# Attention decoder layer: context turned by a DMA transpose per batch, and value products run in pairs

## The chip, the cores and the metric

One core of a Trainium2 chip runs the whole kernel as one program. The metric is the device time in microseconds, the median over several runs. A profile is one more execution, recorded by the hardware profiler.

## The reference

A decoder layer on 16 batches of 56 tokens with 128 features, each with a context of 1500 rows. Cut to what matters here:

```python
x = x + self_attention(layernorm(x))                       # 16 heads of 8
q = heads(layernorm(x) @ Wq.T);  k = heads(ctx @ Wk.T);  v = heads(ctx @ Wv.T)
scores = einsum('bhqd,bhkd->bhqk', q, k) / sqrt(8) + bias[:, None, None, :]   # 16 x 16 x 56 x 1500
x = x + merge(softmax(scores) @ v) @ Wo.T
x = x + experts(layernorm(x))                              # 32 experts, top 4, and a shared one
```

The change touches the cross-attention alone: how the context is turned so that TensorE can project keys and values from it, and in what order the loop over key tiles issues its work.

## The kernel before, in words

The program writes out each engine's instructions by hand, with semaphores between them. SP issues every DMA, on one queue. There are three stages. The first projects queries and keys of the self-attention and prepares batches 0 and 1 of the cross-attention; in it the self-attention runs over 16 batches (`self_step`). The second is the cross-attention, 16 iterations, one per batch (`iteration(r, c)`, batch 3r + c; TensorE, ScalarE, VectorE and SP have one each, batches 1 to 12 in a loop of four rounds of three). The third is the expert layer.

**Preparing a batch.** SP loads 1500 context rows as 12 tiles of 125 rows (`load_ctx`, 750 KB, three buffers). GpSimd (POOL) splits them into two half-precision parts, `ch` (L555 and L558, three buffers). Then nine uses of a PSUM bank follow: T0 to T2, TensorE transposes 2 x 4 blocks of 128 x 128 (`ctx_transpose`, L672) and VectorE copies the bank to `ct` (`take_ctx`, L1323, one buffer); K0 to K2, three matmuls of 500 columns project the keys (L339 to L341 through `split_matmul`), ScalarE copies one half (L1085), VectorE subtracts the other (L1330); V0 to V2, twelve matmuls of 128 columns, a copy by ScalarE (L1089). When K2 is read, SP spreads the keys over the row groups with 12 DMAs (`key_stacks`, L412; the four bias rows, L407, go ahead of them). Batches 0 to 2 are prepared in the first stage, with three banks; batches 3 to 15 in iterations 1 to 13, two batches ahead of use.

**A cross-attention iteration** has 12 steps, one for each tile of 125 keys. In a step TensorE does, in this order: the use of the one bank `misc` that the list `MISC` names for the step (L67: T, K, V, `sel` to pick the heads' outputs of the batch before, `mt` to transpose the maxima of the next batch, `tr` to transpose the result); the scores, four matmuls (L910); one matmul for the maxima of the next batch (L866); the value products of the tile before, eight matmuls in fp32 (`times_v`, L767 and L770); a second matmul for the maxima (L866). The next batch's maxima are computed ahead in 24 such products, over two banks (`mbank`), each reduced by VectorE (L1506); they become a row that is added to the scores. For that, TensorE transposes them (`mt`, L903), ScalarE copies the row (L1166), and SP writes it into the queries with a DMA (L462). The first scores of a batch wait for that DMA (`mrow_in`). The scores of a tile go to one of two banks (`sbank`), ScalarE takes the exponential into one of two buffers `p` (L1171, bias per key), and the value products read it. ScalarE does the `misc` use of a step first and the exponential after it; VectorE the `misc` use first and the two maxima after it.

**SP in an iteration** waits until POOL has split the batch three ahead, loads its context, waits for the scores of the last batch, loads the queries (L423) and stacks the keys of the batch two ahead, and sends the row of maxima.

Of the kernel before, what the change touches and what calls it, by code (L numbers as in the profile page):

```python
# [38 lines left out]
G = 4  # L39
# [23 lines left out]
PREP = ["T0", "T1", "T2", "K0", "K1", "K2", "V0", "V1", "V2"]  # L63
# [3 lines left out]
MISC = ["T0", "K0", "T1", "K1", "T2", "K2", "sel", "V0", "V1", "V2", "mt", "tr"]  # L67


TAIL = {(B - 2, "T0"): "out", (B - 2, "K2"): "norm", (B - 1, "T0"): "logits"}  # L70
OFFSET = {"T": 2, "K": 2, "V": 2, "s": -1, "t": -1, "m": 1}
# [13 lines left out]
def used(r, c, use):  # L85

    return (prep_live if use[0] in "TKV" else live)(r, c + OFFSET[use[0]]) or tail(r, c, use) is not None
# [7 lines left out]
def misc_index(r, c, use):  # L95

    if not isinstance(r, int) and c < 1:
        return misc_index(r, c + 3, use) - 3 * len(MISC)
# [3 lines left out]
    return n if isinstance(r, int) else n + 3 * len(MISC) * r  # L102

# [34 lines left out]
def build(nc, x_d, ctx_d, bias_d, qkv_w, qkv_b, proj_w, proj_b, wq, wk, wv, wo,  # L138
          wg, w1, w2, w3, ws1, ws2, ws3, out_d):
    with ExitStack() as stack:  # L140
# [49 lines left out]
        ch = [sb(f"ch{n}", [128, 2, KT, D], F16) for n in range(3)]  # L190
        ct = sb("ct", [128, 2, KT, 128], F16)
# [7 lines left out]
        p = [sb(f"p{n}", [128, H * S], F32) for n in range(2)]  # L199
        mx = sb("mx", [112, 8, 3], F32)  # L200
# [84 lines left out]
        prep_read = {u: sem(f"prep_read{u}") for u in "TKV"}  # L285
# [11 lines left out]
        ch_ok = sem("ch_ok")  # L297
        k1_ok = sem("k1_ok")
# [55 lines left out]

        def use_bank(r, c, j):
# [8 lines left out]
        def _(sp):  # L364
# [26 lines left out]

            def query_stacks(n, k):
# [34 lines left out]
            query_stacks(0, 0)  # L427
            query_stacks(0, 1)
# [3 lines left out]
            load_ctx(0, 3)  # L432
            sp.wait_ge(mselfr_ok, 1)
# [4 lines left out]

# [30 lines left out]
            with sp.Fori(0, 4, 1) as r:  # L469
# [40 lines left out]
        def _(pool):  # L510
# [32 lines left out]
            def split_ctx(r, c):  # L543
# [5 lines left out]
                if not isinstance(r, int) or b >= 3:  # L549

                    if isinstance(r, int):
                        pool.wait_ge(*use_filled(r, c - 3, "T2"))
                    else:
                        pool.wait_ge(misc_done, misc_index(r, c - 4, "T0"))
                nc.gpsimd.tensor_tensor(ch[n][:, 0], ctx[n][:], zero[:].to_broadcast([128, KT, D]), ALU.add  # L555
                                        ).then_inc(ch_step, 1)
                pool.wait_ge(ch_step, b + 1)
                nc.gpsimd.tensor_tensor(ch[n][:, 1], ctx[n][:], ch[n][:, 0], ALU.subtract).then_inc(ch_ok, 1)  # L558
# [71 lines left out]
        def _(pe):  # L630
# [30 lines left out]
            def ctx_transpose(r, c, j):  # L661

                if not early(r, c):
                    pe.wait_ge(misc_read, batch_index(r, c, f"T{j}"))
                elif 3 * r + c:
                    pe.wait_ge(*use_read(r, c - 1, f"V{j}"))
                pe.wait_ge(ch_ok, 3 * r + c + 1)
                bank = use_bank(r, c, j).bitcast(F16)
                for part in range(2):
                    for t in range(4):  # L670
                        o = 512 * part + 128 * t
                        last = tr(bank[:, o:o + 128], ch[c % 3][:, part, 4 * j + t], identh[:])  # L672
                last.then_inc(use_filled(r, c, "T0")[0], 1)

            def key_project(r, c, j):

                if early(r, c):
                    pe.wait_ge(*use_read(r, c, f"T{j}"))
                else:
                    pe.wait_ge(misc_read, batch_index(r, c, f"K{j}"))  # L680
                c1, c2 = ct[:, 0, 4 * j:4 * j + 4, 0:KP], ct[:, 1, 4 * j:4 * j + 4, 0:KP]
# [4 lines left out]
            def value_project(r, c, j):  # L686
# [4 lines left out]
                for t in range(4):  # L691
                    last = split_matmul(use_bank(r, c, j)[0:KP, 128 * t:128 * t + 128],
                                        ct[:, 0, 4 * j + t, 0:KP], ct[:, 1, 4 * j + t, 0:KP],
# [3 lines left out]
            prepare = {"T": ctx_transpose, "K": key_project, "V": value_project}  # L697
# [38 lines left out]
            for use in PREP[0:6]:  # L736
                prepare[use[0]](0, 0, int(use[1]))
# [7 lines left out]
            for use in PREP[6:]:  # L745
# [4 lines left out]
            for use in PREP[0:3]:  # L750
                prepare[use[0]](0, 1, int(use[1]))
# [5 lines left out]
            for use in PREP[3:]:  # L757
# [88 lines left out]
            for use in PREP[0:6]:  # L846
# [22 lines left out]
            def pv_tile(r, c, t):  # L869
# [3 lines left out]
                if t == 0:  # L873
# [3 lines left out]
                    else:  # L877
                        pe.wait_ge(misc_read, misc_index(r, c, "T0"))
                    pe.wait_ge(o_read, B + 3 * r + c)
                times_v(v[c % 3][:, t], p[t % 2], KP, t == 0, t == KT - 1)  # L880

            def iteration(r, c):
                for s in range(KT):
                    use = MISC[s]
                    if used(r, c, use):
                        if use[0] in "TKV" and not tail(r, c, use):
                            prepare[use[0]](r, c + 2, int(use[1]))
                        else:
                            pe.wait_ge(misc_read, misc_index(r, c, use))
                        if tail(r, c, use) == "out":  # L890
                            out_project(1, 0, misc, misc_done)
                        if tail(r, c, use) == "norm":
                            transpose_norm(2, 0, 6, misc_done)
                        if tail(r, c, use) == "logits":
                            router_logits(0, misc).then_inc(misc_done, 1)
                        if use == "sel":
                            pe.wait_ge(o_read, B + 3 * r + c)
                            pick_heads()
                        elif use == "tr":
                            tr(misc[:, 0:128], tok[:], ident[:]).then_inc(misc_done, 1)  # L900
                        elif use == "mt":
                            pe.wait_ge(mcol_ok, 3 * r + c + 2)
                            tr(misc[0:8, 0:112], mcol[:], ident[0:112, 0:112]).then_inc(misc_done, 1)  # L903
                    if live(r, c):
                        if s == 0:
                            pe.wait_ge(mrow_in[c % 3], 16 * (r + c // 3 + 1))

                        pe.wait_ge(exp_done, B + KT * (3 * r + c) + s - 1)
                        for g in range(G):
                            last = mm(sbank[s % 2][0:KP, g // 2, 224 * (g % 2):224 * (g % 2) + 224],  # L910
                                      ks[c % 3][0:ROWS, g, KP * s:KP * s + KP],
                                      qsb[c % 3][0:ROWS, HG * g:HG * g + HG].rearrange("p h q -> p (h q)"),
                                      start=True, stop=True)
                        last.then_inc(st_done, 1)
                    (off0, k0), (off1, k1) = chunks(s)
# [692 lines left out]
```

## Time and profile before

| | |
|---|---|
| Time, median of 3 runs | 643.82 us (643.49 to 644.13) |
| Profiled execution: span of its instructions | 640.8 us |
| Share of the span in which TensorE is busy | 89% |
| VectorE | 71% |
| ScalarE | 53% |
| GpSimd | 25% |
| Mean granted TensorE clock | 0.928 |
| Mean DMA traffic | 70 GB/s |

The profiled execution counts from its first instruction to its last; the measured time holds some 3 us more, around the span. Matmuls are pipelined: the length of one in the trace is longer than the distance between two, so what an instruction costs TensorE is read from the starts. SPq is the queue of SP, and its lengths are those of the issue, not of the transfer. A line in brackets after an instruction says how long its engine was idle before it and what ended that.

### The profile page before, as it was taken

How to read it: one execution, taken by the hardware profiler on the slowest of the kernel's cores; microseconds unless marked ns; L12 is line 12 of the kernel's file. 1: busy time of each engine (PE TensorE's matmuls, PEld its weight loads, DVE VectorE, ACT ScalarE, POOL GpSimd, SP SyncE). 2: the span in 40 equal slices, each digit the busy share in tenths (PEclk: the TensorE clock that was granted, in tenths of full speed). 3: DMA queues.
4: the chain of work that ended last, by engine and by line, in shares of the span. 5: the costliest groups of instructions: out<-in, count | busy, mean ns of one | idle time of the engine just before them, and what ended most of it. 6: DMA issues, size and time to landing. Idle time of an engine off the chain costs nothing.

```text
span 640.8 us, 18136 instructions
## 1 busy us (share of the span) xinstructions
PE 569.6 (89%) x6656; PEld 368.7 (58%) x6656; DVE 458.0 (71%) x879; ACT 342.0 (53%) x509; POOL 162.4 (25%) x105
## 2 busy tenths in 40 slices
PE   3588887588999997999979999799999999689996
PEld 2267665344676774767747677476776666334442
DVE  6954435977888784787747878488788873478885
ACT  2630654314666663666636666366666668235553
POOL 6895000400033033030330303303030004025540
PEclk9975999775999997999969999799999999789999
DMA  4473300143432432224322243222421304002200
GB/s 108 151 143 111 77 0 2 35 103 72 106 79 72 120 77 73 68 68 122 78 70 62 74 116 78 76 57 79 116 79 26 74 2 101 1 13 50 49 0 29
DMA packets 45473, 45.12 MB, mean 70 GB/s; under 512 B 30387, under 2 KB 37259, under 8 KB 45403
## 3 DMA queue, kind: packets, MB, share of 16 engines
q1 hardware_dynamic: 45403, 44.07, 26.2%
q8 instruction: 58, 0.95, 0.6%
q14 instruction: 12, 0.10, 0.1%
HBM read 16.82 MB, written 0.46 MB: 27 GB/s over the span
## 4 chain that ended last, share of the span: by engine, by line
PE 75%; DVE 8%; issue 6%; POOL 5%; DMA 2%; ACT 2%; SPq 1%; ACTq 0%; DVEq 0%; POOLq 0%
PE ps L866 16%; PE ps L767 12%; PE ps L910 11%; PE ps L339 6%; PE ps L340 5%; PE ps L341 5%; PE ps L672 4%; PE ps L975 3%; PE ps L770 3%; PE ps L777 2%; PE ps L729 2%; DVE mx L1506 2%; DMA ctx<-in_ctx 2%; PE ps L960 1%; DVE xn L1252 1%
## 5 line engine op out<-in xcount | busy, mean ns | idle before, releaser
L1506 DVE TENSOR_REDUCE mx<-ps 112x1 f32<-112x500 f32 x384 | 251.0, 673 | 54.3 <-PE ps L866 52.3
L1171 ACT ACTIVATE p<-ps,bres 125x896 f32<-125x896 f32 x192 | 193.1, 1006 | 92.7 <-PE ps L910 91.9
L866 PE MATMUL ps<-ks,qsb 97*112 97x500 f16 x384 | 160.4, 420 | 11.4 <-DVE mx L1506 10.9
L555 POOL TENSOR_TENSOR ch<-ctx,zero 128x1536 f16<-128x1536 f32 x16 | 43.9, 2745 | 286.2 <-DMA ctx<-in_ctx 286.2
L910 PE MATMUL ps<-qsb,ks 98*125 98x224 f16 x768 | 109.9, 266 | 0.0
L767 PE MATMUL ps<-p,v 125*27 125x168 f32 x1664 | 105.8, 322 | 4.4 <-issue 2.8
L910 PEld LDWEIGHTS ps<-qsb,ks 98*125 98x125 f16 x768 | 83.3, 140 | 14.3 <-issue 2.1
L866 PEld LDWEIGHTS ps<-ks,qsb 97*112 97x112 f16 x384 | 50.6, 132 | 41.5 <-DVE mx L1506 21.5
L767 PEld LDWEIGHTS ps<-p,v 125*27 125x27 f32 x1664 | 31.8, 105 | 59.7 <-issue 53.5
L770 PE MATMUL ps<-p,v 125*9 125x56 f32 x1664 | 60.5, 215 | 0.0
L770 PEld LDWEIGHTS ps<-p,v 125*9 125x9 f32 x1664 | 47.1, 92 | 11.1
L1330 DVE TENSOR_TENSOR k<-ps,k 128x500 f16<-128x500 f32 x48 | 32.4, 677 | 29.1 <-ACT k L1085 29.1
L558 POOL TENSOR_TENSOR ch<-ctx,ch 128x1536 f16<-128x1536 f32 x16 | 50.4, 3149 | 1.3
L1085 ACT ACTIVATE k<-ps 128x500 f16<-128x500 f32 x48 | 28.2, 588 | 36.5 <-PE ps L341 36.4
L672 PE MATMUL ps<-identh,ch 128*128 128x128 f16 x384 | 32.1, 236 | 15.1 <-issue 10.9
L1089 ACT ACTIVATE v<-ps 125x512 f32<-125x512 f32 x48 | 28.4, 596 | 27.9 <-PE ps L341 27.7
L1323 DVE COPY ct<-ps 128x1024 f16<-128x1024 f16 x48 | 32.6, 682 | 13.4 <-PE ps L672 13.2
L672 PEld LDWEIGHTS ps<-identh,ch 128*128 128x128 f16 x384 | 26.2, 107 | 23.7 <-issue 14.1
L339 PE MATMUL ps<-wt,ct 128*125 128x128 f16 x192 | 37.0, 227 | 0.0
L341 PE MATMUL ps<-wt,ct 128*125 128x128 f16 x192 | 36.9, 226 | 0.0
L340 PE MATMUL ps<-wt,ct 128*125 128x128 f16 x192 | 36.9, 226 | 0.0
L612 POOL TENSOR_TENSOR ks<-ks,zero 128x384 f16<-128x384 f32 x17 | 19.7, 1158 | 59.2 <-PE ps L975 40.4
(172 smaller groups left out, 799.9 us busy)
## 6 DMA issues: line engine op xcount, KB each, us to landing
ks<-k SPq DMA_DIRECT2D x192, 93.8 KB
ctx<-in_ctx SPq DMA_DIRECT2D x16, 750.0 KB
ks<-in_L_ffn_W SPq DMA_DIRECT2D x48, 64.0 KB, 2.0
qsb<-qs SPq DMA_DIRECT2D x15, 168.0 KB, 7.7
qs<-late SPq DMA_DIRECT2D x8, 168.0 KB, 4.1
ks<-brow SPq DMA_DIRECT2D x64, 2.9 KB
qs<-late SPq DMA_DIRECT2D x16, 56.0 KB, 2.9
qs<-late SPq DMA_DIRECT2D x8, 112.0 KB, 2.5
```

What stands on the lines that cost most here:

```text
L339: nc.tensor.matmul(out, a1, b1, start=True, stop=False)
L340: nc.tensor.matmul(out, a1, b2, start=False, stop=False)
L341: return nc.tensor.matmul(out, a2, b1, start=False, stop=True)
L555: nc.gpsimd.tensor_tensor(ch[n][:, 0], ctx[n][:], zero[:].to_broadcast([128, KT, D]), ALU.add).then_inc(ch_step, 1)
L558: nc.gpsimd.tensor_tensor(ch[n][:, 1], ctx[n][:], ch[n][:, 0], ALU.subtract).then_inc(ch_ok, 1)
L672: last = tr(bank[:, o:o + 128], ch[c % 3][:, part, 4 * j + t], identh[:])
L767: mm(obank[32 * quad:32 * quad + 27, 0:168], vt[0:keys, 27 * quad:27 * quad + 27], pt[0:keys, 168 * quad:168 * quad + 168], start=first, s ...
L770: done = mm(obank[32 * quad:32 * quad + 9, 168:224], vt[0:keys, 108 + 9 * quad:117 + 9 * quad], pt[0:keys, 672 + S * quad:672 + S * quad + ...
L866: mm(mbank[k % 2][0:112, 0:CH], qsb[n][0:ROWS - 1, 2 * pair:2 * pair + 2].rearrange("p h q -> p (h q)"), ks[n][0:ROWS - 1, pair // 2, CH * ...
L910: last = mm(sbank[s % 2][0:KP, g // 2, 224 * (g % 2):224 * (g % 2) + 224], ks[c % 3][0:ROWS, g, KP * s:KP * s + KP], qsb[c % 3][0:ROWS, HG ...
L1171: A(p[s % 2][0:KP].rearrange("p (a c) -> p a c", a=2), sbank[s % 2][0:KP, :, 0:448], ACT.Exp, scale=SCALE, bias=bres[:, bass.ds(i, 1), s:s ...
L1506: V.tensor_reduce(mx[:, k // 3, k % 3:k % 3 + 1], mbank[k % 2][0:112, 0:CH], axis=AX.X, op=ALU.max).then_inc(mx_read, 1)
```

## The change

The context is turned by one DMA per batch. `ctx_transpose` and `take_ctx` go, with the T uses of the `misc` bank. SP issues `dma_start_transpose` from `ch` to `ct`; `ct` has three buffers, `ch` one, so POOL splits a batch only when the transposition of the batch before has landed, and SP issues a transposition only when the last one has landed. In an iteration it stands behind the load of the queries and ahead of the key stacks, for the batch three ahead; the context load goes four ahead. SP's loop is written out. `MISC` keeps 12 places, three of them empty. Value products run in odd steps only, for the two tiles before the last one, with three buffers `p` (the third lies in `wnat`). In a step TensorE now does the value products, the scores, the first maxima product, the `misc` use and the second maxima product; ScalarE does the exponential before the `misc` use, VectorE the maxima before it.

```diff
-PREP = ["T0", "T1", "T2", "K0", "K1", "K2", "V0", "V1", "V2"]
+PREP = ["K0", "K1", "K2", "V0", "V1", "V2"]
-MISC = ["T0", "K0", "T1", "K1", "T2", "K2", "sel", "V0", "V1", "V2", "mt", "tr"]
+MISC = ["", "K0", "", "K1", "", "K2", "sel", "V0", "V1", "V2", "mt", "tr"]
...
-        ch = [sb(f"ch{n}", [128, 2, KT, D], F16) for n in range(3)]
-        ct = sb("ct", [128, 2, KT, 128], F16)
+        ch = sb("ch", [128, 2, KT, D], F16)
+        ct = [sb(f"ct{n}", [128, 2, KT, 128], F16) for n in range(3)]
...
+        p.append(wnat[:].rearrange("p n d -> p (n d)")[:, 0:H * S])
...
+            def transpose_ctx(r, c):
+                if not live(r, c):
+                    return
+                n, b = c % 3, 3 * r + c
+                sp.wait_ge(ch_ok, b + 1)
+                if not isinstance(r, int) or b > 0:
+                    sp.wait_ge(*ct_landed(r, c - 1))
+                if isinstance(r, int) and 3 <= b < 3 + EARLY:
+                    sp.wait_ge(*use_filled(r, c - 3, "V2"))
+                elif not isinstance(r, int) or b >= 3:
+                    sp.wait_ge(misc_done, misc_index(r, c - 3, "K0"))
+                sp.dma_start_transpose(out=ct[n][:].rearrange("p a t k -> p (a t) k"),
+                                       in_=ch[:].rearrange("p a t d -> p (a t d)")).then_inc(ct_ok[n], 16)
...
             query_stacks(0, 0)
+            transpose_ctx(0, 0)
             query_stacks(0, 1)
...
             key_stacks(0, 0)
             load_ctx(0, 3)
+            transpose_ctx(0, 1)
...
             key_stacks(0, 1)
+            transpose_ctx(0, 2)
...
# SP, iteration(r, c)
-                if not isinstance(r, int) or 3 * r + c >= 1:
-                    load_ctx(r, c + 3)
+                if not isinstance(r, int) or 3 * r + c >= 0:
+                    load_ctx(r, c + 4)
                 if prep_live(r, c + 2):
                     sp.wait_ge(st_done, B + KT * (3 * r + c))
                     load_queries(r, c + 2)
+                if not isinstance(r, int) or 3 * r + c >= 0:
+                    transpose_ctx(r, c + 3)
+                if prep_live(r, c + 2):
                     key_stacks(r, c + 2)
...
-            with sp.Fori(0, 4, 1) as r:
+            for r in range(4):
...
# POOL, split_ctx
+                if not isinstance(r, int) or b > 0:
+                    pool.wait_ge(*ct_landed(r, c - 1))
...
# TensorE
-            for use in PREP[0:6]:
+            for use in PREP[0:3]:
                 prepare[use[0]](0, 0, int(use[1]))
...
             self_maxima(0)
-            for use in PREP[0:3]:
-                prepare[use[0]](0, 1, int(use[1]))
...
             def iteration(r, c):
                 for s in range(KT):
+                    (off0, k0), (off1, k1) = chunks(s)
+                    if s % 2:
+                        for t in (s - 3, s - 2):
+                            if live(r, c if t >= 0 else c - 1):
+                                pv_tile(r, c if t >= 0 else c - 1, t % KT)
                     if live(r, c):
+                        scores(r, c, s)
                     if live(r, c + off0):
                         max_chunk(r, c, off0, k0)
-                    if s == 0 and live(r, c - 1):
-                        pv_tile(r, c - 1, KT - 1)
-                    if s > 0 and live(r, c):
-                        pv_tile(r, c, s - 1)
+                    misc_use(r, c, s)
                     if live(r, c + off1):
                         max_chunk(r, c, off1, k1)
...
# ScalarE, iteration: now ahead of the misc use
+                    if live(r, c):
+                        tile = B + KT * i + s
+                        act.wait_ge(st_done, tile + 1)
+                        act.wait_ge(pv_done, tile - 2)
+                        A(p[s % 3][0:KP].rearrange("p (a c) -> p a c", a=2), sbank[s % 2][0:KP, :, 0:448],
...
+                    if s == 1 and live(r, c - 1):
+                        act.wait_ge(pv_done, B + KT * i)
+                        A(osb[:], obank[:, 0:224], ACT.Copy).then_inc(o_read, 1)
```

## Rows read from the trace of the kernel before

**Rows 1.** The chain that ended last, shares of the span by line.

```profile
PE ps L866 16%; PE ps L767 12%; PE ps L910 11%; PE ps L339 6%; PE ps L340 5%; PE ps L341 5%; PE ps L672 4%; PE ps L975 3%; PE ps L770 3%; PE ps L777 2%; PE ps L729 2%; DVE mx L1506 2%; DMA ctx<-in_ctx 2%; PE ps L960 1%; DVE xn L1252 1%
```

**Rows 2.** Busy time by stretch: length, busy per engine, clock, DMA share, GB/s.

```profile
171.00:195.00 24.00, 23.91 (x347) 16.52 (x340) 19.50 (x35) 15.45 (x22) 5.86 (x2) 1.00 0.32 90
...
322.10:354.40 32.30, 27.81 (x341) 18.06 (x340) 19.67 (x34) 15.53 (x21) 5.84 (x2) 0.84 0.24 68
...
378.60:403.20 24.60, 24.60 (x349) 17.15 (x349) 20.08 (x36) 16.14 (x23) 5.86 (x2) 1.00 0.32 88
```

**Rows 3.** Timeline of PE, two steps: start us, length us, instruction, count, [idle before].

```profile
303.34 0.62 PE L672 MATMUL ps<-identh,ch 128*128 128x128 f16 x8
...
303.79 0.55 PE L910 MATMUL ps<-qsb,ks 98*125 98x224 f16 x4
...
304.18 0.38 PE L866 MATMUL ps<-ks,qsb 97*112 97x500 f16 x1
...
304.49 0.49 PE L767 MATMUL ps<-p,v 125*27 125x168 f32 x8
...
304.79 0.28 PE L770 MATMUL ps<-p,v 125*9 125x56 f32 x8
...
305.00 0.42 PE L866 MATMUL ps<-ks,qsb 97*112 97x500 f16 x1
...
305.26 0.38 PE L339 MATMUL ps<-ct,wt 128*128 128x500 f16 x1
...
305.90 0.55 PE L910 MATMUL ps<-qsb,ks 98*125 98x224 f16 x4
...
307.45 0.62 PE L672 MATMUL ps<-identh,ch 128*128 128x128 f16 x8
```

**Rows 4.** Timeline of VectorE and ScalarE in the same two steps.

```profile
304.48 1.01 ACT L1171 ACTIVATE p<-ps,bres 125x896 f32<-125x896 f32 x1 [1.01 <-PE ps L910]
...
304.97 1.25 DVE L1506 TENSOR_REDUCE mx<-ps 112x1 f32<-112x500 f32 x2
...
306.10 0.59 ACT L1085 ACTIVATE k<-ps 128x500 f16<-128x500 f32 x1 [0.61 <-PE ps L341]
...
306.72 0.68 DVE L1330 TENSOR_TENSOR k<-ps,k 128x500 f16<-128x500 f32 x1 [0.50 <-ACT k L1085]
```

**Rows 5.** Timeline of ScalarE in batch 0, steps without preparation.

```profile
164.45 1.01 ACT L1171 ACTIVATE p<-ps,bres 125x896 f32<-125x896 f32 x1 [0.46 <-PE ps L910]
165.91 1.01 ACT L1171 ACTIVATE p<-ps,bres 125x896 f32<-125x896 f32 x1 [0.46 <-PE ps L910]
```

**Rows 6.** Timeline around the row of maxima, PE, ScalarE and SP's queue.

```profile
311.54 9.12 SPq L412 DMA_DIRECT2D ks<-k  x12
...
320.10 0.26 PE L903 MATMUL ps<-ident,mcol 112*8 112x112 f32 x1
...
320.40 0.25 ACT L1166 ACTIVATE mrow<-ps 8x112 f16<-8x112 f32 x1
...
320.77 0.68 SPq L462 DMA_DIRECT2D qsb<-mrow  x1
```

**Rows 7.** DMA queue, then issues: KB each, median us to landing.

```profile
q1 hardware_dynamic: 45403, 44.07, 26.2%
...
qsb<-qs SPq DMA_DIRECT2D x15, 168.0 KB, 7.7
...
qsb<-late SPq DMA_DIRECT2D x8, 14.0 KB, 1.8
```

**Rows 8.** Timeline of SP's queue and of PE, first stage.

```profile
31.30 1.28 SPq L400 DMA_DIRECT2D qs<-late  x2
...
54.90 0.48 SPq L386 DMA_DIRECT2D ctx<-in_ctx  x1
...
63.30 0.62 PE L339 MATMUL ps<-ct,wt 128*128 128x500 f16 x1
```

**Rows 9.** Timeline of SP's queue, end of the late query stacks.

```profile
163.58 1.70 SPq L400 DMA_DIRECT2D qs<-qd  x1
```

More of the change, by code:

```diff
@@ L85, in used @@
 def used(r, c, use):
-    return (prep_live if use[0] in "TKV" else live)(r, c + OFFSET[use[0]]) or tail(r, c, use) is not None
+    if not use:
+        return False
+    return (prep_live if use[0] in "KV" else live)(r, c + OFFSET[use[0]]) or tail(r, c, use) is not None
 def tail(r, c, use):
@@ L297, in build @@
         ch_ok = sem("ch_ok")
+        ct_ok = [sem(f"ct_ok{n}") for n in range(3)]
         k1_ok = sem("k1_ok")
@@ L659, in out_project, with key_project @@
                 last.then_inc(done, 1)
-            def ctx_transpose(r, c, j):
+            def key_project(r, c, j):
                 if not early(r, c):
-                    pe.wait_ge(misc_read, batch_index(r, c, f"T{j}"))
+                    pe.wait_ge(misc_read, batch_index(r, c, f"K{j}"))
                 elif 3 * r + c:
                     pe.wait_ge(*use_read(r, c - 1, f"V{j}"))
[L667 to L681, printed above, removed]
+                if j == 0:
+                    pe.wait_ge(*ct_landed(r, c))
+                c1, c2 = ct[c % 3][:, 0, 4 * j:4 * j + 4, 0:KP], ct[c % 3][:, 1, 4 * j:4 * j + 4, 0:KP]
                 out = use_bank(r, c, j)[:, 0:CH].rearrange("p (t k) -> p t k", t=4)
@@ L744, in _ @@
             last.then_inc(bt_psum, 1)
-            for use in PREP[6:]:
+            for use in PREP[3:]:
                 prepare[use[0]](0, 0, int(use[1]))
@@ L756, in _ @@
             tr(ps[:, 0, 0:112], mself[:].rearrange("p b k -> p (b k)"), ident[0:112, 0:112]).then_inc(mselft_psum, 1)
-            for use in PREP[3:]:
+            for use in PREP:
                 prepare[use[0]](0, 1, int(use[1]))
@@ L845, in _ @@
             pe.wait_ge(x_ok, 1)
-            for use in PREP[0:6]:
+            for use in PREP[0:3]:
                 prepare[use[0]](0, 2, int(use[1]))
@@ new lines, in scores @@
+            def scores(r, c, s):
+                if s == 0:
+                    pe.wait_ge(mrow_in[c % 3], 16 * (r + c // 3 + 1))
+                pe.wait_ge(exp_done, B + KT * (3 * r + c) + s - 1)
+                for g in range(G):
+                    last = mm(sbank[s % 2][0:KP, g // 2, 224 * (g % 2):224 * (g % 2) + 224],
+                              ks[c % 3][0:ROWS, g, KP * s:KP * s + KP],
+                              qsb[c % 3][0:ROWS, HG * g:HG * g + HG].rearrange("p h q -> p (h q)"),
+                              start=True, stop=True)
+                last.then_inc(st_done, 1)
@@ L882, in iteration @@
             def iteration(r, c):
                 for s in range(KT):
[L884 to L903, printed above, removed]
@@ L904, in iteration @@
-                    if live(r, c):
[L905 to L914, printed above, removed]
@@ L926, in _ @@
             transpose_norm(1, 1, 2, xt_psum)
-            for use in PREP[6:]:
+            for use in PREP[3:]:
                 prepare[use[0]](0, 2, int(use[1]))
@@ L1093, in _ @@
             take = {"K": take_keys, "V": take_values}
-            for use in PREP[3:6]:
+            for use in PREP[0:3]:
                 take[use[0]](0, 0, int(use[1]))
@@ L1102, in _ @@
             act.wait_ge(ones_ok, 1)
-            for use in PREP[6:]:
+            for use in PREP[3:]:
                 take[use[0]](0, 0, int(use[1]))
@@ L1106, in _ @@
             A(mrow_self[:], ps[:, 0, 0:112], ACT.Copy, scale=1.0 / BIG).then_inc(mselfr_ok, 1)
-            for use in PREP[3:]:
+            for use in PREP:
                 take[use[0]](0, 1, int(use[1]))
@@ L1142, in _ @@
                 self_step(5, c)
-            for use in PREP[3:6]:
+            for use in PREP[0:3]:
                 take[use[0]](0, 2, int(use[1]))
@@ L1147, in _ @@
             act.wait_ge(pv_done, B)
-            for use in PREP[6:]:
+            for use in PREP[3:]:
                 take[use[0]](0, 2, int(use[1]))
@@ L1418, in _ @@
             norm_stats(1, 1)
+            norm_apply(1, 1)
             for use in PREP[0:3]:
-                take[use[0]](0, 2, int(use[1]))
-            norm_apply(1, 1)
-            for use in PREP[3:6]:
                 take[use[0]](0, 2, int(use[1]))
```

107 lines of the change are left out of this document (55 added, 52 removed).

## The prediction, made before the kernel was built

> **What bounds the kernel now.** I read the chain of waits first: its largest shares are TensorE lines of the cross-attention loop, with the transposes (L672) at 4% and the value products (L767, L770) at 15% [rows 1]. Then the busy times by stretch: a batch with preparation takes 24.0 to 24.6 us, TensorE is busy nearly all of it, VectorE 19.5 to 20.1 us, at the full clock [rows 2]. Three batches are like the one of 32.3 us shown: the same work plus a halt of TensorE at the loop's jump and a lower granted clock, mean 0.84 [rows 2]. Then the timeline of two steps [rows 3]: a step is a list of starts on TensorE. Transposes 0.45 us, four score products 0.39, first maxima product 0.31 (with the change to the value products), value products 0.51, second maxima product 0.26: 1.92 in all. A key step has 0.64 in place of 0.45 and takes 2.19, of which 0.08 is a wait for the `misc` bank. TensorE waits for almost nothing, so work taken from it counts in full, as long as nothing else becomes late.
>
> **Part 1, the transposes.** 39 groups of 8 leave TensorE in the 13 batches prepared in the loop: 3 x 0.45, and 3 x 0.08 of bank waits, 1.6 us a batch. VectorE loses three copies of some 0.68 us; it has idle time, so that alone is worth nothing. In their place comes one DMA of 768 KB per batch, and the trace shows none like it. Lower bound of its time: 1.8 us, the smallest landing [rows 7]. Upper: all DMA time is 26.2% of 16 engines over 640.8 us for 45403 packets, 59 ns each [rows 7]; 128 rows x 24 pieces of 256 bytes are 3072 packets, 192 an engine, 11.3 us. I take 5, near the 7 us of a context load of 750 KB (the queries issued behind one land 7.7 us after their issue [rows 7]) and of better spread. How long SP's queue is held is unseen too: between 0.5 us (one load [rows 8]) and the full 11; I take 3. In the steady state both lie beside other work: the transposition is issued one batch ahead, POOL's split needs 6 us of a 24-us batch, and SP is idle from the bias rows until the keys (K2) are read.
>
> The row only allows bounds, and the Trainium skill has two rules. DMA: Bandwidth & Descriptors (Latency and other measured facts) gives 261 GB/s for a DMA transpose with a strided middle dimension: 3.0 us, an estimate; by it the sum would hardly change. VectorE: DVE Perf Modes (The three transpose paths) gives 1309 ns for one 128x128 block through the DMA crossbar: 24 of them would be 31.4 us a batch, an estimate. No row bears on either.
>
> **Part 2, the order.** Value products of two tiles run together. One of the two entries (0.31 instead of 0.21 to 0.26) goes. Inside a tile the second set of four starts 0.30 after the first, when its 0.28 us are hardly over [rows 3], so I take the first tile at 0.42 (0.30 + 0.12) and the last at 0.51. Bounds for the pair: 0.80 to 1.10 us; I take 0.93. With the entries that is about 0.17 us a pair, 1.0 a batch. Work removed in a prepared batch: 1.6 + 1.0 = 2.6 us.
>
> What comes back as waits, worked out by walking the new order with these durations:
> - Maxima in bursts. Two banks; a reduction holds VectorE 0.60 us when the next one is ready (two take 1.25), and a product is readable 0.41 us after its start [rows 3, 4]. An even step with no `misc` use (s = 0, 2, 4) is 0.39 + 0.21 + 0.30 = 0.90 us on TensorE, so its second product stands before a bank still being read: 0.25 us, 0.7 a batch.
> - The selection of heads (s = 6) needs the bank of K2 (s = 5). K2's copy now stands behind the exponential on ScalarE (starts 0.69 after the scores, 1.01 long), its subtraction behind two maxima on VectorE [rows 4]: after K2's start the exponential ends at 0.94, the copy at 1.56, the maxima in front at 1.66, the subtraction at 2.36; wanted after 0.64 + 0.26 + 0.39 + 0.26 = 1.55. Wait 0.8 us.
> - The row of maxima. Now its transpose is at 320.10, the copy at 320.40, the DMA at 320.77 [rows 6], and the next batch's first scores come 0.1 + 1.47 + 0.1 + 1.47 + 0.45 = 3.6 us after the transpose: it is in time. After the change the copy stands behind the exponential: ready 1.2 us after the transpose, issued 0.1 later, landed 1.8 to 2.6 later (14 KB land in 1.8 [rows 7]); and TensorE is at the next scores after 0.1 + 0.30 + 0.93 + 0.39 + 0.26 + 0.11 + 0.26 = 2.35 us, as the scores are now first in the batch. Wait 0.8 to 1.5 us; I take 0.8. Everything on TensorE is queued behind it. SP is no later: the 12 key DMAs take 9.1 us [rows 6] and end just before the copy.
>
> 2.6 - 0.7 - 0.8 - 0.8 = 0.3 us gained a batch, 13 batches: **-4**.
>
> Batches without preparation only lose. Batch 0 runs at 1.46 us a step [rows 5], 2.92 a pair. In bursts: from the first maxima product of an odd step, the reductions of its pair end 0.41 + 0.60 + 0.68 = 1.7 later, then the fourth product, and 0.30 + 0.93 + 0.39 to the next: 3.3 to 3.4. Five such pairs: **+2**. Batch 14 has as many and batch 15, with value products one step later at its end, loses about 1: **+3** together.
>
> **Part 3, the stages ahead.** SP's queue is passed by the transpositions. The first goes out at 31.3, ahead of the second set of query DMAs [rows 8], which so move by the 3 us it holds the queue; the self maxima wait for them. The second follows the key stacks and the context load, issued at 54.90 now [rows 8], about 58 then, and its data come behind that load: landed at 66 to 70. K0 of batch 1 starts at 63.30 now [rows 8]; it would start about 68. **+5**, bounds 0 and +10. The copies of batch 2's transposes lie under VectorE's wait for POOL's split: nothing. In batch 0 SP is busy with late query stacks until 165.3 [rows 9]; then come a context load and a transposition, and only then the row of maxima for batch 1; in the kernel before the row goes ahead of that load. It lands some 7 + 3 us after 165.3, at 176; wanted at 173. **+3**, bounds 0 and +7. SP's unrolled loop adds code and no wait. The three halts at TensorE's loop jump run beside a context load as before: 0, between -1 and +3 each if a transposition delays the code.
>
> Sum: -4 + 2 + 3 + 5 + 3 = +9 on 640.8 us of span. The median of the runs is 643.8, 3.0 more than the span; that stays: 652.8, say 653.
>
> **Rivals.**
> - Faster. The pair of value products costs 0.80 and the waits at s = 6 and at the next batch's scores are half of mine: a prepared batch gains 0.3 + 6 x 0.13 + 0.8 = 1.9 at best, 1.4 if VectorE, now pressed harder, takes 0.5 back. 13 x 1.4 = 18; of the 13 lost elsewhere 5 go with the same waits at the edges, 8 stay: 634. For it: TensorE's removed work is certain, my waits are differences of small numbers. Against it: the row's copy behind a 1-us exponential. It decides at 1 us gained per prepared batch, which pays the 13 lost elsewhere.
> - Transposition slow, holding SP 11 us (the upper row bound). In each batch SP would reach the keys at 1.2 + 11 + 3.2 (four bias-row DMAs at 0.8) = 15.4 us, where K2 is read at 12.1 (two pairs of 3.6, an even step of 0.9, 1.6 to K2, 2.4 for it): 3.3 us late for keys and row, 13 x 3.3 = +43 on my sum: 696. Nothing in the rows excludes it. By the Trainium skill's figure (VectorE: DVE Perf Modes, as above) a transposition would hold SP 20 us longer still, and 13 times that would bring the time near 960, an estimate; its chance lies within this rival's.
> - Break-even: the start costs 1 instead of 8, the rest as I sum it: 644 to 646.
>
> **Chances.** Forecast (646 to 672) 0.55, faster 0.30, break-even 0.10, slow transposition 0.05. About 0.2% (1.3 us) is what a measurement of this kernel can tell from no change. Faster by more 0.30, within 0.08, slower 0.62. The range 632 to 672 leaves out the slow transposition, part of the fast case, and the forecast's upper end (a row landing in 2.6 us adds 10, a pair at 1.10 adds 14).
>
> **What would show it.** No transposes of `ch` on TensorE and no `ct` copies on VectorE. A prepared batch at 23.5 to 24 us, batch 0 and 14 some 2 us longer. New waits: L910 at the batch's first scores for a DMA, L777 for VectorE's subtraction of K2, L866 for the maxima. K0 of batch 1 at 66 to 70. The forecast is wrong if a prepared batch takes under 23.2 us, if the scores of a batch don't wait for the row, or if the transposition takes over 11 us.

## The result and the profile after

The changed kernel takes 662.35 us (median of four runs, 658.04 to 667.98) against 643.79 us before; the ratio is 1.0266, 95% interval 1.0228 to 1.0304. The ratio leaves out the run of 667.98 us, which was a slow execution; the middle of the other three is 660.7 us, and that is what later runs are compared with. The change is slower by 17 us where 9 were forecast (653), and inside the range. The profiled execution took 660.73 us, its span is 659.0 us, 18.2 more than the span before, so the steps below are read from it.

The page of the changed kernel: span, busy time of the engines, the DMA queue, and the chain that ended last, by engine and by line.

```profile
span 659.0 us, 17150 instructions
...
PE 544.7 (83%) x6272; PEld 351.7 (53%) x6272; DVE 427.3 (65%) x831; ACT 337.0 (51%) x509; POOL 162.4 (25%) x105
...
q1 hardware_dynamic: 95067, 56.66, 45.0%
...
PE 53%; issue 12%; DVE 12%; SPq 11%; DMA 7%; ACT 3%; POOL 2%; ACTq 0%; DVEq 0%; POOLq 0%
PE ps L877 10%; PE ps L778 8%; PE ps L923 8%; PE ps L344 6%; SPq L424 5%; DVE mx L1490 5%; PE ps L345 5%; PE ps L346 5%; DMA qsb<-mrow 4%; PE ps L995 3%; SPq L436 3%; PE ps L781 2%; PE ps L788 2%; SPq L413 2%; DMA ct<-ch 2%
```

The DMA queue carries 95067 packets instead of 45403, and its time goes from 26.2% to 45.0% of the 16 engines [rows 7]. In the chain, SP's queue has 11%, DMA 7% and VectorE 12%; TensorE is down to 53%, from 75% before. Something other than TensorE now sets the end in many places.

I cut both kernels at the first scores of each batch, read from TensorE's timeline (us):

| stretch | before | changed |
|---|---|---|
| start to batch 0 | 149.1 | 156.5 |
| batch 0 | 22.7 | 29.6 |
| batches 1 to 13 together | 337.5 | 339.0 |
| batch 14 | 21.2 | 24.9 |
| batch 15 and the rest | 110.3 | 109.0 |
| span | 640.8 | 659.0 |

So of +18.2, +7.4 is the start, +6.9 batch 0, +1.5 thirteen prepared batches, and +2.4 batch 14 and the rest. From the last value products on, where the change touches nothing, it is 95.2 us before and 93.4 here, so the attention's part of that +2.4 is about 4. Windows of three batches of the changed kernel (columns as in [rows 2]):

```profile
211.50:239.60 28.10, 23.76 (x319) 16.06 (x319) 18.41 (x33) 15.85 (x23) 5.85 (x2) 0.94 0.59 105
478.30:501.80 23.50, 22.07 (x320) 15.38 (x320) 17.86 (x32) 15.32 (x22) 0.00 (x0) 1.00 0.40 93
525.15:550.03 24.88, 20.58 (x280) 14.39 (x280) 16.42 (x39) 13.75 (x19) 1.02 (x1) 0.93 0.01 2
```

The middle one is a prepared batch without disturbance: 23.5 us, against 24.0 to 24.2 before, from first scores to first scores. The first has the same work and takes 28.1, at a granted clock of 0.94 and with 59% of DMA time. The third is batch 14. Now what TensorE waited for in the changed kernel: us in total, times, longest.

```profile
PE ps L923 <- issue: 20.5, 7, 4.3
PE ps L877 <- DVE mx L1490: 16.9, 47, 7.0
PE ps L344 <- DMA ct<-ch: 14.9, 2, 11.8
PE ps L923 <- DMA qsb<-mrow: 12.0, 12, 6.7
PE ps L788 <- DVE k L1343: 8.8, 13, 0.8
```

"issue" at L923 is the largest and is 7 waits. Its records, with others that I use below, from TensorE's timeline (start, length, instruction, count, idle before):

```profile
186.11 1.00 PE L923 MATMUL ps<-qsb,ks 98*125 98x224 f16 x4 [6.67 <-DMA qsb<-mrow]
...
224.11 0.35 PE L923 MATMUL ps<-qsb,ks 98*125 98x224 f16 x2 [2.94 <-issue]
...
225.03 0.62 PE L345 MATMUL ps<-ct,wt 128*128 128x500 f16 x1
...
318.81 0.49 PE L778 MATMUL ps<-p,v 125*27 125x168 f32 x8
...
319.71 0.50 PE L923 MATMUL ps<-qsb,ks 98*125 98x224 f16 x3
...
461.96 0.35 PE L923 MATMUL ps<-qsb,ks 98*125 98x224 f16 x2 [2.66 <-issue]
```

The first line is the start of batch 1: TensorE stood 6.67 us for the row of maxima. The second is the middle of a group of scores in batch 2, where nothing of the program is waited for; 2.94 us are lost, and the key products behind it take 0.62 us where they take 0.38 at the full clock [rows 3]: from 224.1 to 228.0 the granted clock was 0.56, with stretches at the lower of its two levels, and from 228.0 on 1.00. The next two are the pair of value products (0.90 us from its start to the next scores). The last is another halt inside a group of scores; two more, of 1.21 us each, end at 303.77 and 381.97. SP's queue around batches 0 to 2, with how long each issue held it:

```profile
171.22 0.62 SPq L424 DMA_DIRECT2D qs<-qd  x1
171.88 0.51 SPq L395 DMA_DIRECT2D ctx<-in_ctx  x1
172.52 9.54 SPq L413 DMA_TRANSPOSE ct<-ch  x1
182.11 0.72 SPq L491 DMA_DIRECT2D qsb<-mrow  x1
...
191.85 3.00 SPq L413 DMA_TRANSPOSE ct<-ch  x1
...
209.66 0.67 SPq L491 DMA_DIRECT2D qsb<-mrow  x1
210.37 0.46 SPq L395 DMA_DIRECT2D ctx<-in_ctx  x1
210.96 0.55 SPq L447 DMA_DIRECT2D qsb<-qs  x1
211.62 8.84 SPq L413 DMA_TRANSPOSE ct<-ch  x1
```

A transposition that is issued behind a context load (172.52, 211.62) holds SP's queue 9.54 and 8.84 us; one with none just ahead (191.85) holds it 3.00. Of all 16, four held it 3.0 to 3.8 us, all with no load just ahead, and the twelve behind a load 8.8 to 10.1. When the row of maxima for batch 1 was ready, and when POOL, which waits for the landing, began its next split after two of the transpositions (those of 172.52 and 211.62):

```profile
177.44 0.24 ACT L1196 ACTIVATE mrow<-ps 8x112 f16<-8x112 f32 x1
...
185.91 2.75 POOL L580 TENSOR_TENSOR ch<-ctx,zero 128x1536 f16<-128x1536 f32 x1 [56.99 <-DMA ct<-ch]
...
224.53 2.75 POOL L580 TENSOR_TENSOR ch<-ctx,zero 128x1536 f16<-128x1536 f32 x1 [22.01 <-DMA ct<-ch]
```

The row is ready at 177.68 and leaves at 182.11, when the hold is over: 4.4 us late. It is in at 186.11, 4.0 us later, at about the time when the transposition ahead of it has landed (185.91).

### The profile page after: what moved, and what is told of

It reads as the page before. It is cut to its first block, busy times and chain, and to the rows that moved or that the text cites. A ratio compares the mean times of both kernels' runs of the same rounds, so it can differ in the third digit from the quotient of the medians.

```text
span 659.0 us, 17150 instructions
## 1 busy us (share of the span) xinstructions
PE 544.7 (83%) x6272; PEld 351.7 (53%) x6272; DVE 427.3 (65%) x831; ACT 337.0 (51%) x509; POOL 162.4 (25%) x105
## 2 busy tenths in 40 slices
DMA packets 95135, 57.66 MB, mean 87 GB/s; under 512 B 80051, under 2 KB 86923, under 8 KB 95067
## 3 DMA queue, kind: packets, MB, share of 16 engines
q1 hardware_dynamic: 95067, 56.66, 45.0%
## 4 chain that ended last, share of the span: by engine, by line
PE 53%; issue 12%; DVE 12%; SPq 11%; DMA 7%; ACT 3%; POOL 2%; ACTq 0%; DVEq 0%; POOLq 0%
PE ps L877 10%; PE ps L778 8%; PE ps L923 8%; PE ps L344 6%; SPq L424 5%; DVE mx L1490 5%; PE ps L345 5%; PE ps L346 5%; DMA qsb<-mrow 4%; PE ps L995 3%; SPq L436 3%; PE ps L781 2%; PE ps L788 2%; SPq L413 2%; DMA ct<-ch 2%
## 5 line engine op out<-in xcount | busy, mean ns | idle before, releaser
L1179 ACT ACTIVATE p<-ps,bres 125x896 f32<-125x896 f32 x128 | 128.6, 1007 | 122.1 <-PE ps L923 121.5
L923 PE MATMUL ps<-qsb,ks 98*125 98x224 f16 x768 | 117.1, 277 | 32.5 <-issue 20.5
L923 PEld LDWEIGHTS ps<-qsb,ks 98*125 98x125 f16 x768 | 84.8, 143 | 59.1 <-issue 37.3
L1179 ACT ACTIVATE wnat<-ps,bres 125x896 f32<-125x896 f32 x64 | 64.6, 1009 | 46.2 <-PE ps L923 45.8
L778 PE MATMUL ps<-p,v 125*27 125x168 f32 x1152 | 68.9, 321 | 1.3 <-ACT p L1179 0.6
L781 PE MATMUL ps<-p,v 125*9 125x56 f32 x1152 | 41.7, 218 | 0.0
L781 PEld LDWEIGHTS ps<-p,v 125*9 125x9 f32 x1152 | 32.9, 94 | 8.1
L569 POOL TENSOR_TENSOR rstd<-veps,mhalf 128x4 f32<-128x4 f32 (+1 forms) x6 | 5.7, 957 | 121.8 <-DVE veps L1265 121.8
L344 PE MATMUL ps<-ct,wt 128*128 128x500 f16 x48 | 20.7, 431 | 16.9 <-DMA ct<-ch 14.9
L778 PEld LDWEIGHTS ps<-p,v 125*27 125x27 f32 x1152 | 23.6, 107 | 20.6 <-issue 13.2
L778 PE MATMUL ps<-wnat,v 125*27 125x168 f32 x512 | 32.3, 326 | 0.5 <-ACT wnat L1179 0.5
```

Source lines behind the costliest of these rows:

```text
L344: nc.tensor.matmul(out, a1, b1, start=True, stop=False)
L778: mm(obank[32 * quad:32 * quad + 27, 0:168], vt[0:keys, 27 * quad:27 * quad + 27], pt[0:keys, 168 * quad:168 * quad + 168], start=first, s ...
L781: done = mm(obank[32 * quad:32 * quad + 9, 168:224], vt[0:keys, 108 + 9 * quad:117 + 9 * quad], pt[0:keys, 672 + S * quad:672 + S * quad + ...
L1179: A(p[s % 3][0:KP].rearrange("p (a c) -> p a c", a=2), sbank[s % 2][0:KP, :, 0:448], ACT.Exp, scale=SCALE, bias=bres[:, bass.ds(i, 1), s:s ...
```

## Experiments

Eight kernels ran. Beside them the kernel before gave 643.3 and 643.4 us.

### The order of load and transposition

```diff
-            load_ctx(0, 3)
             transpose_ctx(0, 1)
+            load_ctx(0, 3)
...
-                    load_ctx(r, c + 4)
...
                     transpose_ctx(r, c + 3)
+                    load_ctx(r, c + 4)
```

> The changed kernel with each transposition issued ahead of the context load that stood before it (three places on SP's queue). Theory (a transposition that is queued behind a 750 KB load holds SP until that load has drained): SP is held 3 to 4 us by every transposition instead of 9 to 10, the wait for the first row of maxima in batch 0 falls from 6.7 us to under 1.5, K0 of batch 1 no longer waits, the row waits of 0.4 us in later batches stay (they come from the late copy, not from SP); 662 - 6 - 3 = 652 to 655. Rival 1 (the hold of 9 us is the transposition's own time when other traffic runs): still 8 to 10 us, time 659 or more. Rival 2 (SP sets the period of the prepared batches in the changed kernel): also 0.5 us less in each of 13 batches, 645 to 648.

Measured: 644.8 us, ratio to before 1.0011 (0.9979 to 1.0044). The exchange of two issues takes 16 us off the changed kernel's 660.7, more than any of the cases expected; the theory's 652 to 655 was missed. The transposition's own rows in this run (ns shortest, median, longest; then us to landing), and TensorE's waits:

```profile
L413 SPq DMA_TRANSPOSE ct<-ch x16: 3090/3303/4943, 30.1 to 459.4; - x16
...
DMA to landing us min/median/max: 4.7/6.1/8.3
```

```profile
PE ps L922 <- issue: 12.0, 3, 4.5
PE ps L344 <- DMA ct<-ch: 11.9, 1, 11.9
PE ps L922 <- DMA qsb<-mrow: 9.9, 12, 5.0
```

The hold is 3.3 us at the median and 4.9 at most, so rival 1 is out; a transposition lands 6.1 us after its issue (12.4 in the changed kernel). The 3.1 us wait for `ct` at the first stage is gone (14.9 in two waits became 11.9 in one). "issue" fell from 20.5 in 7 waits to 12.0 in 3: only the three halts at the loop's jump are left. For rival 2, that SP sets the period, the batches count whose transposition stands behind a load. The changed kernel has two with no other disturbance than a halt of 1.21 us: 24.9 us, 23.7 without the halt, against 23.6 here. The rival's 0.5 us a batch is not there. One part of my theory failed: the wait for the first row fell from 6.7 to 5.0 us only. The experiment on the first row of maxima takes that up.

By the two profiles the exchange is worth 3.1 us in the start, 1.6 in batch 0 and 14.0 in the thirteen prepared batches (339.0 became 325.1; before it was 337.5). Of the 14.0, 8.0 are the four halts inside the bodies and 0.4 those at the jump; the other 5.6 were not taken apart. Behind batch 14 this profile is 5.5 us longer, mostly because batch 15 ran at a granted clock of 0.74 instead of 1.00; one profile can't say whether that belongs to the edit.

### Each part alone

Part 1 alone, the transposition behind its load, the loop bodies of TensorE, VectorE and ScalarE as before. Against the changed kernel, main lines only:

```diff
-        p.append(wnat[:].rearrange("p n d -> p (n d)")[:, 0:H * S])
...
-                times_v(v[c % 3][:, t], p[t % 3], KP, t == 0, t == KT - 1)
+                times_v(v[c % 3][:, t], p[t % 2], KP, t == 0, t == KT - 1)
...
-                    misc_use(r, c, s)
+                    if s == 0 and live(r, c - 1):
+                        pv_tile(r, c - 1, KT - 1)
+                    if s > 0 and live(r, c):
+                        pv_tile(r, c, s - 1)
```

> Part 1 alone: context transposed by DMA as in the changed kernel, but the old order in a step and one value product per step, two probability buffers. Theory (the order gives nothing, the transposition takes 1.6 us of TensorE's work away but SP then needs 23.2 us a batch: 0.7 + 0.5 + 0.6 + 9 + 3.6 + 8.8): prepared batches 23.2 to 23.4 instead of 24.1, 13 x -0.8 = -10, start +7, batch 0 +5, halts for code +3: 646 to 650. Rival (the transposition itself is what costs, the order helps): 656 or more.

Measured: 645.5 us, ratio 1.0022 (0.9988 to 1.0055), just under the theory's range; the rival is out. But not by the way I reckoned. Its profiled execution was 7.4 us above the median, so its lengths are read with care. An undisturbed prepared batch takes 23.3 us, as the theory has it, but the next experiment, where SP is held 3 to 5 us only, gives the same 23.3: SP is not what sets it. One transposition on SP's queue and the halt of TensorE at the loop's jump:

```profile
258.76 8.74 SPq L412 DMA_TRANSPOSE ct<-ch  x1
267.36 1.00 PE L956 MATMUL ps<-qsb,ks 98*125 98x224 f16 x4 [8.21 <-issue]
```

SP is held until 258.76 + 8.74 = 267.50, and TensorE goes on at 267.36, after 8.21 us in which it waited for nothing of the program. At the same jump before it stood 2.9 us, and 1.8 a little later. The three halts at the jumps are 21.2 us together, and there is none of the four that the changed kernel has inside its bodies.

Then the same kernel with each transposition ahead of its load, by the exchange of the first experiment:

> Part 1 alone, with each transposition ahead of the load. Theory: SP needs 17.5 us a batch and is no bound, prepared batches fall to TensorE's own 22.4 to 22.6 us, 13 x -1.6 = -21, start +4, batch 0 +1: 626 to 632, faster than both kernels. Rival (the transpositions slow the key, query and code transfers by sharing the DMA engines, whatever their place): prepared batches 23.3 or more, 640 or more.

Measured: 635.0 us, ratio 0.9869 (0.9821 to 0.9918): faster than before, slower than I expected of it, and between the theory and the rival. The three halts at the jump are 12.3 us together. The prepared batch is 23.3 us (23.1 where no context is loaded and split any more), not 22.4. That is the rival's number for the batch, but not its cause: without the load it is still 23.1, so sharing the DMA engines is worth 0.2 at most. Two steps of TensorE tell why:

```profile
457.54 0.38 PE L875 MATMUL ps<-ks,qsb 97*112 97x500 f16 x1
...
458.36 0.42 PE L875 MATMUL ps<-ks,qsb 97*112 97x500 f16 x1
458.62 0.55 PE L955 MATMUL ps<-qsb,ks 98*125 98x224 f16 x4
459.29 0.42 PE L875 MATMUL ps<-ks,qsb 97*112 97x500 f16 x1
```

The step with nothing in `misc` begins at 458.62, and its first maxima product stands 0.67 us behind the scores, where it takes 0.39 otherwise [rows 3]: VectorE has not read the bank. Of the 0.53 us that go with one group of transposes, 0.28 come back as a wait for the maxima; a batch gains 3 x 0.25 or a little more, not 1.6; by its length, 24.2 to 23.3, it is 0.9.

Part 2 alone, transposes on TensorE, new order, pairs of value products, three probability buffers. Against the kernel before, main lines only:

```diff
-                times_v(v[c % 3][:, t], p[t % 2], KP, t == 0, t == KT - 1)
+                times_v(v[c % 3][:, t], p[t % 3], KP, t == 0, t == KT - 1)
...
+                    if s % 2:
+                        for t in (s - 3, s - 2):
+                            if live(r, c if t >= 0 else c - 1):
+                                pv_tile(r, c if t >= 0 else c - 1, t % KT)
                     if live(r, c):
-                        if s == 0:
...
+                        scores(r, c, s)
```

> Part 2 alone: the transposes stay on TensorE, the new order in a step, value products in pairs, three probability buffers. Theory (pairing gives 1.0 us a batch and its waits take more: 0.8 at the selection of heads, 0.4 at the row of maxima, some at the maxima's banks): prepared batches 24.2 to 24.6, +1 to +4 over 13, batches 0, 14 and 15 +5: 649 to 654. Rival (the order gives more than it takes): 642 or less.

Measured: 669.5 us, ratio 1.0406 (1.033 to 1.0482). The sign was right, the size not: an undisturbed prepared batch takes 26.2 us, 2.0 more than before. TensorE's waits:

```profile
PE ps L673 <- DVE k L1340: 21.7, 26, 1.1
PE ps L867 <- DVE mx L1491: 11.9, 25, 4.9
PE ps L778 <- DVE k L1340: 9.8, 13, 0.8
PE ps L913 <- DMA qsb<-mrow: 9.1, 13, 3.5
```

21.7 us are waits of the transposes (L673) for VectorE's subtraction of the keys, 26 of them: T1 and T2 in 13 batches. The wait that I had reckoned for the selection alone (L778, 0.8 each) stands behind K0 and K1 too, because whatever follows a key projection in the next step finds the bank unread: its copy is behind the exponential, its subtraction behind two maxima. The parts do not add up: +2 and +26 us apart, +17 together. The new order needs the steps that the transposes left empty.

### The first row of maxima

Part 1 alone with the transposition first still waited 4.4 us at the start of batch 1. SP's queue there, and the scores:

```profile
166.59 3.08 SPq L412 DMA_TRANSPOSE ct<-ch  x1
169.71 0.48 SPq L394 DMA_DIRECT2D ctx<-in_ctx  x1
171.57 0.72 SPq L489 DMA_DIRECT2D qsb<-mrow  x1
...
178.37 2.75 POOL L578 TENSOR_TENSOR ch<-ctx,zero 128x1536 f16<-128x1536 f32 x1 [53.30 <-DMA ctx<-in_ctx]
...
178.65 0.78 PE L955 MATMUL ps<-qsb,ks 98*125 98x224 f16 x4 [4.44 <-DMA qsb<-mrow]
```

The row is issued at 171.57, as soon as it is copied, and is in at 178.65, 7.1 us later; in the prepared batches of the changed kernel it takes 1.8 (209.66 to 211.49, the wait's end). Its 1.8 KB stand behind the transposition's 768 KB and the load's 750 KB, and that load has landed just before the row: POOL starts on its context at 178.37.

```diff
             iteration(0, -1)
+            transpose_ctx(0, 3)
+            load_ctx(0, 4)
             query_stacks(1, 1)
             query_stacks(1, 2)
```

> Part 1 alone with each transposition ahead of its load, and besides the transposition of batch 3 and the load of batch 4 ahead of the late query stacks, so that in batch 0 nothing stands before the row of maxima but those stacks. Theory (the row's 1.8 KB wait behind the 768 KB of the transposition and the 750 KB of the load in the DMA engines; in the run without this edit it landed 7 us after its issue, against 1.8 elsewhere): the wait of 4.4 us at the first scores of batch 1 goes, 635 - 4 = 630 to 632. Rival (the late query stacks behind the pair move the row instead): SP reaches the row later, gain under 1.5 us.

Measured: 628.0 us, ratio 0.9781 (0.9722 to 0.984), better than the theory's 630 to 632. The wait for the row is gone altogether, batch 0 is back at 22.4 us, and the time falls by 7.0, of which 4.4 is that wait. Batch 1, which followed the wait at a granted clock of 0.93 and now runs at 1.00, falls by another 1.6 (24.9 to 23.3). The row leaves when it is ready, so the rival is out.

### The unevenness of the new order

From the kernel of the first experiment (transposition first) on:

```diff
-MISC = ["", "K0", "", "K1", "", "K2", "sel", ...
+MISC = ["K0", "", "K1", "", "K2", "", "sel", ...
```

> The changed kernel with each transposition ahead of its load, and the key projections moved from the odd steps (1, 3, 5, where the pair of value products also is) to the even ones (0, 2, 4, which the transposes left empty). Theory (the new order loses by unevenness: odd steps of 2.4 us beside even ones of 0.9 leave VectorE late, and K2 directly before the selection leaves the bank unread): the wait of 0.76 us at the selection and the two of 0.17 us at the maxima go, and the weight-load waits for maxima with them; prepared batch 23.5 down to 22.4 to 22.8, 13 x -0.9 = -12: 630 to 636. Rival (VectorE's maxima, two of 0.68 us a step, bound the batch whatever the order): under 0.3 us a batch, 641 or more.

Measured: 640.8 us, ratio 0.9949 (0.9925 to 0.9973), 4.0 below the first experiment, between theory and rival. TensorE's waits:

```profile
PE ps L876 <- DVE mx L1489: 20.4, 66, 6.2
PE ps L922 <- DMA qsb<-mrow: 13.6, 13, 5.1
PE ps L344 <- DMA ct<-ch: 11.7, 1, 11.7
```

No row is left for the selection (it was 9.9 us in 13 waits), but the waits for maxima grew from 16.6 in 46 to 20.4 in 66, and the batch is 23.0 to 23.1, from 23.5 to 23.6. The selection's wait was real, and removing it shows the maxima as the next one.

> As the run before, and on ScalarE the copy of the row of maxima stands ahead of the exponential of its step. Theory (the row comes late because its copy waits for the exponential): the row waits of 0.4 us and more go, another 0.4 to 1.0 us a batch: 13 x 0.6 = 8 below the run before, 622 to 629. Rival (the row is late because the last maxima are, so the copy starts hardly earlier): within 2 us of the run before.

```diff
+                    if MISC[s] == "mt" and used(r, c, "mt"):
+                        act.wait_ge(misc_done, misc_index(r, c, "mt") + 1)
+                        A(mrow[:], misc[0:8, 0:112], ACT.Copy, scale=1.0 / BIG).then_inc(misc_read, 1)
                     if live(r, c):
                         tile = B + KT * i + s
```

Measured: 637.8 us, ratio 0.9915 (0.989 to 0.994). The row waits of the later batches, 0.36 to 0.39 us each, are gone, so the copy behind the exponential made the row late; the batch falls to 22.8, 3 us in all, not the 8 expected.

> As the run before, and the transposition of batch 3 and the load of batch 4 ahead of the late query stacks. Theory: 4 to 5 us below the run before, from the first scores of batch 1: 618 to 625, the fastest of all. Rival: no difference.

Measured: 630.3 us, ratio 0.9789 (0.975 to 0.9828), 7.4 below the run before, much the same step (7.0) as this edit made in part 1 alone. It missed the 618 to 625 and was not the fastest of all. Windows of the last prepared batch but one and of batch 14, first for part 1 alone with both edits of SP's queue (628.0 us), then for this kernel:

```profile
449.20:472.40 23.20, 22.94 (x321) 15.43 (x320) 18.17 (x32) 15.81 (x22) 0.00 (x0) 1.00 0.40 94
495.50:516.70 21.20, 19.02 (x282) 13.09 (x280) 16.35 (x38) 13.20 (x18) 1.02 (x1) 1.00 0.01 2
```

```profile
448.20:471.10 22.90, 22.34 (x321) 15.50 (x321) 17.90 (x32) 15.55 (x22) 0.00 (x0) 1.00 0.41 95
493.80:518.90 25.10, 21.40 (x282) 14.65 (x280) 16.77 (x39) 13.47 (x18) 1.02 (x1) 0.86 0.01 1
```

From first scores to first scores the pairs win 0.3 to 0.5 us in each undisturbed prepared batch (22.8 against 23.1 to 23.3) and 3.2 over all 13, and lose 3.9 in batch 14, where the work without preparation comes in bursts and the granted clock is 0.86 instead of 1.00, 1.6 in batch 0 (24.0 against 22.4) and 0.9 in batch 15. Their intervals overlap: with the queue in order, the pairs are worth nothing that these runs can tell.

## Why the prediction was right, and where it was not

**Transposes off TensorE, 1.6 a batch.** The work went, but VectorE took 0.28 back in each emptied step. I had such a wait (0.25, 0.7 a batch) in the list for the new order; it comes already with the empty step, in the old order.

**The pair.** Taken 0.93, measured 0.90.

**Waits of a prepared batch.** Selection: 0.8 said, 0.76 seen on TensorE (8.8 us in 13). Row of maxima: 0.8 said, 0.4 seen; the row lands 1.8 us after its issue as taken, the sum ahead of it was off by less than half a microsecond. Maxima: 0.7 said, and 0.7 seen if it is read from the starts: in two of the empty steps the second product starts 0.55 us behind the first instead of 0.21 (the profile lists only 0.17 of each as idle, because the lengths of matmuls overlap). A prepared batch thus gained 2.6 - 0.7 - 0.8 - 0.4 = 0.7 instead of 0.3: 23.5 us, as "23.5 to 24" had it, and 13 of them would have given -9 instead of -4.

**The transposition is hidden in the steady state.** This is the step that failed. I took 3 us of hold and put the upper bound at 11. Alone the hold is 3.0 to 3.8; behind the load, where the change puts it, 8.8 to 10.1. I costed the wrong one, and looked for the price in the keys alone: SP reaches them at 0.7 + 0.5 + 0.6 + 8.8 + 3.8 = 14 us, which still just does. The price came elsewhere, as halts of TensorE in which it waits for nothing of the program. Four of them in the middle of bodies, 2.94 + 1.21 + 1.21 + 2.66 = 8.0 us, stand in the changed kernel and in none of the six kernels with the transposition first; my sum had 0 for the halts (between -1 and +3 each, at the jumps alone). The kernel before had two of its own shortly behind the jumps (1.76 and 0.86), and its jumps took 10.9 against 12.4, so all halts together rose by 7, from 13.5 to 20.5.

Two of the four end 0.4 us before POOL's split, which waits for the landing of a transposition, begins (224.11 and 224.53, 461.96 and 462.33), the other two 1.7 before it; those at the jumps end well before a landing. That TensorE's code is loaded behind the load and the transposition is my reading, and the trace has no row for it; what the runs show is that the order of the two issues makes and unmakes the halts, with the same bytes. -9 and +7 leave -2; measured +1.5. In the rest are batch 1 (25.4 us), which began behind the row's wait, a row that came 0.88 late in batch 3, and the granted clock behind the longer halts (the batches that follow those at the jumps ran at 0.89 to 0.90, the two with only 1.21 us of halt at 1.00); I did not separate them.

**Batch 0, +5 (2 + 3).** Measured +6.9, of which the row's wait 6.67. The bursts cost 0.2, not 2: 29.6 - 6.7 = 22.9 against 22.7. The row was late by the hold, which was 9.5 where I had 3 and kept it back by 4.4 us, and then by data, 4.0 us to land. From the end of the query stacks to its landing I had 7 + 3 = 10 us; it took 14.3 (171.84 to 186.11). The hold is not the whole of it: with one of 3.2 or 3.1 us the row left when it was ready and still took 6.8 to 7.1 us to land, and in the first experiment the wait was still 5.0.

**Start, +5.** Measured +7.4. K0 of batch 1 came at 68.70 ("about 68"), after 3.06 us for `ct`; the second set of queries kept the self maxima waiting 2.3. With the transposition first the start is 153.4, so 3.1 of the 7.4 were the order. Of the remaining 4.3 my sum overlooked the first batch: its K0 starts at 36.12, after 11.8 us of waiting for the first transposition, where it started at 32.79 with the transposes on TensorE, 3.3 us later. No run changed that place, so how much of it reaches the end of the stage is not shown.

**Batches 14 and 15, +3.** Measured +3.7 for batch 14, of which 1.4 is a wait for the row of batch 15, and +0.5 for batch 15 up to its last value products; the unchanged last stage happened to be shorter.

So the sign came from the right places, start, batch 0 and end, with +13 said and +16.7 measured, and the loop between them gained 4 in my sum and lost 1.5 in fact. That the result lies inside the range is in part luck: its upper end was made of a row landing later in every prepared batch and a dearer pair, and neither came; the long hold, which did come, I had only in the rival at 696, priced by late keys. One more term was read wrongly. I added 3.0 us from span to time; every run on record has 1.7 to 1.8 (660.73 against 659.0), so the kernel before was profiled in an execution of some 642.5, 1.3 us below its median.

The number of the break-even, to which I gave a tenth, is what one exchange of two lines made of the change, though by other terms: the start still costs 4.3, and the loop gains 12.5. "Faster", at 634, did not happen: of its conditions only the row's wait was half of mine.

**How long a transposition takes.** The 3.0 us worked out from the rate in the Trainium skill's DMA: Bandwidth & Descriptors (Latency and other measured facts) is for the transfer. In the first experiment the shortest landing was 4.7 us after the issue, and the packets of one took 4.0 us of all 16 engines; the hold of 3.0 to 3.8 us is near the figure, but it is a different thing. The figure for one block in the Trainium skill's VectorE: DVE Perf Modes (The three transpose paths), which I multiplied to 31.4 us for a batch, is not borne out: a transposition of 24 blocks landed 4.7 to 8.3 us after its issue when it went first.

## What to carry to other kernels

A DMA transposition is worth the place it has in the queue: ahead of the bulk load it cost 3.3 us of the issuing queue, behind it 9, and that order alone moved this kernel by 16 us. Before bulk transfers go into a queue, look at what small or unseen thing stands behind them: here a row of 1.8 KB and, as it seems but is not shown, TensorE's code. An engine relieved of work gives the gain only until the next one is late: 1.6 us of transposes became 0.9, since in every emptied step VectorE's maxima gave 0.28 us back as a wait.

## What I had not expected of the hardware

- The issue of a DMA transposition holds the queue's issuer, 8.8 to 10.1 us behind a 750 KB load and 3.0 to 3.8 with none in the changed kernel (3.1 to 4.9 in the first experiment); a plain load holds it 0.5. It looks as if what is queued ahead must run down first: queries issued between load and transposition (210.96) land 8.7 us after their issue at the median, at about 219.7, and the hold ends at 220.46.
- 768 KB transposed are 3104 packets an execution ((95067 - 45403) / 16), near the 3072 reckoned from 256-byte pieces; the queue's time rose by 0.45 x 659.0 - 0.262 x 640.8 = 129 us, 8.0 for each transposition, and only 0.359 x 645.6 - 168 = 64, 4.0 each, with the transposition first. The same packets took half the engines' time.
- TensorE stood for 8.21 us at a loop's jump, waiting for nothing of the program, while such a pair was under way, and 2.9 to 4.4 us at the jumps before. After the jump halts of the changed kernel the granted clock was lower for a while: 0.50 from 267 to 272.
